# Four PSUM banks for the scores and one for the row maxima, formed in nine pieces, in a one-core attention and FFN kernel

## What is computed

```python
xn = _layernorm(x, axis=-1)
...
attn = jnp.einsum('bhqd,bhkd->bhqk', q, k) * scale
causal = jnp.triu(jnp.ones((Tx, Tx), dtype=bool), k=1)
attn = jnp.where(causal[None, None], -jnp.inf, attn)
attn = jax.nn.softmax(attn, axis=-1)
out = jnp.einsum('bhqk,bhkd->bhqd', attn, vh)
...
x = x + _L0_attn_ref(xn, ...) + _L0_ffn_ref(xn, ...)   # the FFN is quantised to 8 bits, with a gelu
```

## Time and profile before

| | us |
|---|---|
| median of 3 runs | 847.81 |
| lowest and highest | 843.24 and 855.21 |
| the profiled execution's own time | 854.1 |
| span of its trace | 852.3 |
| TensorE busy in the span | 768.1 (90%) |
| VectorE, ScalarE, GpSimd busy | 593.3, 494.2, 421.4 |

### The profile page before, as it was taken

The page is one execution under the profiler, slowest core; times in us unless marked ns, Lnnn a source line. Parts: engine busy times, 40 slices in busy tenths (PEclk is TensorE's granted clock), DMA queues, the critical chain, the costliest instruction groups (busy, mean ns, idle before and its releaser), DMA issues.

```text
span 852.3 us, 18026 instructions
## 1 busy us (share of the span) xinstructions
PE 768.1 (90%) x7038; PEld 580.5 (68%) x7038; DVE 593.3 (70%) x1534; ACT 494.2 (58%) x1005; POOL 421.4 (49%) x210
## 2 busy tenths in 40 slices
PE   4994776999999999999999999999999999999866
PEld 3672454667787778777877787778767876777635
DVE  7545985667676777667676767676766776776796
ACT  2541653666656665666466656565666566656753
POOL 3112661366654655555555555555566466640208
PEclk9766575999999999999999999999999999999978
DMA  9535134000100010001000100010000000000002
GB/s 279 169 123 197 50 123 149 2 14 14 39 14 2 2 26 3 14 13 39 14 1 2 28 1 14 15 41 12 1 5 24 1 3 2 1 2 2 13 1 99
DMA packets 20516, 33.07 MB, mean 39 GB/s; under 512 B 2704, under 2 KB 11472, under 8 KB 20304
## 3 DMA queue, kind: packets, MB, share of 16 engines
q1 hardware_dynamic: 19648, 31.34, 11.8%
q10 hardware_dynamic: 784, 0.59, 0.3%
HBM read 21.30 MB, written 10.49 MB: 37 GB/s over the span
## 4 chain that ended last, share of the span: by engine, by line
PE 45%; issue 25%; DVE 22%; ACT 6%; POOL 1%; DMA 1%; SPq 0%; POOLq 0%; DVEq 0%; ACTq 0%
PE psum L1045 40%; DVE p_lo L976 9%; ACT psum L670 3%; PE psum L1217 2%; DVE o_norm L877 2%; ACT p_hi L669 1%; POOL res L508 1%; DVE hid L1025 1%; DVE small L848 1%; DVE junk L848 1%; PE psum L1069 1%; ACT q_hi L594 1%; DVE small L996 1%; DMA acc<-in_L_attn_x 1%; DVE kt_a L941 1%
## 5 line engine op out<-in xcount | busy, mean ns | idle before, releaser
L669 ACT ACTIVATE p_hi<-psum 128x512 f16<-128x512 f32 (+3 forms) x384 | 187.5, 488 | 177.0 <-PE psum L1045 176.5
L848 DVE CUSTOM_DVE_ANT_0 junk<-psum,cmask 128x1024 bf16<-128x1024 f32 (+7 forms) x256 | 188.0, 753 | 129.8 <-issue 129.7
L976 DVE TENSOR_TENSOR p_lo<-psum,p_hi 128x512 f16<-128x512 f32 (+3 forms) x384 | 204.1, 552 | 57.8 <-ACT psum L670 57.5
L451 POOL TENSOR_TENSOR q_swap<-q_raw,sin_sb 32x1024 f32<-32x1024 f32 x31 | 73.3, 2365 | 267.0 <-ACT q_raw L590 266.9
L670 ACT ACTIVATE psum<-psum 128x512 f32<-128x512 f32 (+3 forms) x384 | 187.4, 488 | 0.0
L1045 PE MATMUL psum<-q_hi,k_hi 128*128 128x512 f32 (+2 forms) x384 | 164.3, 428 | 23.3 <-DVE p_lo L976 21.3
L1045 PEld LDWEIGHTS psum<-kv_tok,p_hi 128*128 128x128 f16 x2304 | 117.4, 96 | 37.6 <-issue 20.7
L1045 PE MATMUL psum<-kv_tok,p_hi 128*128 128x65 f16 (+1 forms) x2304 | 141.9, 195 | 0.4 <-DVE p_lo L976 0.4
L1045 PE MATMUL psum<-k_hi,q_hi 128*128 128x512 f32 (+3 forms) x384 | 123.8, 404 | 9.1 <-DVE small L848 9.1
L1045 PE MATMUL psum<-q_lo,k_hi 128*128 128x512 f32 (+2 forms) x384 | 132.0, 344 | 0.0
L1045 PE MATMUL psum<-q_hi,k_lo 128*128 128x512 f32 (+2 forms) x384 | 131.9, 343 | 0.0
(11 more groups left out here) (172 smaller groups left out, 1272.9 us busy)
## 6 DMA issues: line engine op xcount, KB each, us to landing
wq_split<-w_split SPq DMA_DIRECT2D x4, 1024.0 KB, 5.0
wq<-wq_split SPq DMA_DIRECT2D x16, 256.0 KB, 2.7
k_rotated<-k_split SPq DMA_DIRECT2D x8, 512.0 KB, 3.1
acc<-in_L_attn_x SPq DMA_DIRECT2D x4, 512.0 KB, 7.7
ffn_t<-in_L_attn_W_o SPq DMA_DIRECT2D x1, 2048.0 KB, 19.7
w_split<-in_L_ffn_w SPq DMA_DIRECT2D x2, 1024.0 KB, 6.0
k_hi<-k_rotated SPq DMA_DIRECT2D x8, 256.0 KB, 3.7
k_lo<-k_rotated SPq DMA_DIRECT2D x8, 256.0 KB, 4.3
```

What stands on the lines that cost most here:

```text
L451: pool.tensor_tensor(q_swap[0:HR, :], raw[HR:ROPE, :], sin_sb[HR:ROPE, :], ALU.mult)\
L669: act.activation(p_hi[j % PRING][:, o:o + used], src, ACT.Exp, scale=SCALE)
L848: ins = dve.tensor_tensor_reduce(junk[:, o:o + w], pmax[:, o:o + w], cmask[:, T - w:T], 1.0, LOWEST, ALU.add, ALU.max, mcol[:, s % 2, i:i ...
L976: dve.tensor_tensor(p_lo[j % PRING][:, o:o + used], score[c % SBANKS][:, w - used:w], p_hi[j % PRING][:, o:o + used], ALU.subtract).then_i ...
```

## The change

The scores get four banks, so chunk c uses bank c mod 4 and waits for the `p_lo` of chunk c-4. `pmax` shrinks to one bank. The units of maxima become nine pieces of at most 512 columns; a query tile of more than 512 columns is reduced in two pieces, the first of which leaves its result in the new tile `mpart`, from which the second goes on. `MAX_CHUNK` spreads the ten uses over the chunks of a step: after c0, c2, c3, c4, c5 and c6 the pieces u3 to u8 of step n+1, after c8 the transposition (u9), and after c9, c10 and c11 the pieces u0 to u2 of step n+2. In the preparation the ten uses stand in the seven passes as `FIRST_USES` says, two in the passes n = 2, 4 and 6, and three pieces of step 1 follow instead of two units.

```diff
-SBANKS, PRING = 3, 4
+SBANKS, PRING = 4, 4
...
-MAX_UNITS = [[(7, 0)], [(6, 0)], [(5, 0)], [(4, 0)], [(3, 0), (2, CH)], [(1, 0), (0, CH)]]
+MAX_UNITS = [[(7, 0, 0, CH)], [(7, CH, 0, CH)], [(6, 0, 0, CH)], [(6, CH, 0, 3 * P), (0, 0, 3 * P, P)],
+             [(5, 0, 0, CH)], [(5, CH, 0, 2 * P), (1, 0, 2 * P, 2 * P)], [(4, 0, 0, CH)],
+             [(4, CH, 0, P), (2, 0, P, 3 * P)], [(3, 0, 0, CH)]]
...
-MAX_SLOT = {0: (1, 2), 1: (1, 3), 2: (1, 4), 3: (1, 5), 5: (1, 6), 6: (2, 0), 7: (2, 1)}
...
+MAX_CHUNK = {9: (2, 0), 10: (2, 1), 11: (2, 2), 0: (1, 3), 2: (1, 4), 3: (1, 5), 4: (1, 6), 5: (1, 7), 6: (1, 8), 8: (1, 9)}
...
+FIRST_USES = ((0, 1), (2,), (3, 4), (5,), (6, 7), (8,), (9,))
...
-        score, pmax, head, misc = bank[0:3], psum[:, 3 * CH:5 * CH], bank[5:7], bank[7]
+        score, pmax, head, misc = bank[0:4], bank[4], bank[5:7], bank[7]
...
-                for i, o in MAX_UNITS[u]:
-                    w = (i + 1) * P
-                    ins = dve.tensor_tensor_reduce(junk[:, o:o + w], pmax[:, o:o + w], cmask[:, T - w:T], 1.0, LOWEST,
-                                                   ALU.add, ALU.max, mcol[:, s % 2, i:i + 1])
+                for i, k0, o, w in MAX_UNITS[u]:
+                    last = k0 + w == (i + 1) * P
+                    at = T - (i + 1) * P + k0
+                    if last and k0:
+                        dve.wait_ge(S["max_read"], USES * n + u)
+                    ins = dve.tensor_tensor_reduce(junk[:, o:o + w], pmax[:, o:o + w], cmask[:, at:at + w], 1.0,
+                                                   sm["mpart"][:, i:i + 1] if k0 else LOWEST, ALU.add, ALU.max,
+                                                   mcol[:, s % 2, i:i + 1] if last else sm["mpart"][:, i:i + 1])
...
-                pmax_use(0, 0, n - 2)
+                for u in FIRST_USES[n - 2]:
+                    pmax_use(0, 0, u)
...
-            for k in range(2):
+            for k in range(3):
                 pmax_use(1, 1, k)
...
-                            if c == (ENDS[j - 1] if j else 0) and j in MAX_SLOT:
-                                m, u = MAX_SLOT[j]
+                            if c in MAX_CHUNK:
+                                m, u = MAX_CHUNK[c]
...
-                        scores(n, s, j)
-                        if j in MAX_SLOT:
-                            m, u = MAX_SLOT[j]
-                            if n + m < LAST:
-                                if u == 0:
-                                    pe.wait_ge(S["qhi_done"], n + m + 1)
...
-                                pmax_use(n + m, s + m, u)
+                        for c in range(ENDS[j - 1] if j else 0, ENDS[j]):
+                            scores(n, s, c)
+                            if c in MAX_CHUNK:
+                                m, u = MAX_CHUNK[c]
+                                if n + m < LAST:
+                                    if u == 0:
+                                        pe.wait_ge(S["qhi_done"], n + m + 1)
...
+                                    pmax_use(n + m, s + m, u)
```

More of the change, by code:

```diff
@@ L74 @@
 ENDS = [max(c for c, x in enumerate(CHUNKS) if x[0] == j) + 1 for j in range(NT)]
[L75 removed]
+SBANKS, PRING = 4, 4
 LO_BASE = SBANKS
 assert NC % SBANKS == 0 and NT % PRING == 0
[L80 removed]
+MAX_UNITS = [[(7, 0, 0, CH)], [(7, CH, 0, CH)], [(6, 0, 0, CH)], [(6, CH, 0, 3 * P), (0, 0, 3 * P, P)],
+             [(5, 0, 0, CH)], [(5, CH, 0, 2 * P), (1, 0, 2 * P, 2 * P)], [(4, 0, 0, CH)],
+             [(4, CH, 0, P), (2, 0, P, 3 * P)], [(3, 0, 0, CH)]]
 NU = len(MAX_UNITS)
 USES = NU + 1
[L85 to L86 removed]
+MAX_CHUNK = {9: (2, 0), 10: (2, 1), 11: (2, 2), 0: (1, 3), 2: (1, 4), 3: (1, 5), 4: (1, 6), 5: (1, 7), 6: (1, 8), 8: (1, 9)}
+assert [u for _, u in sorted((m * -NC + c, u) for c, (m, u) in MAX_CHUNK.items())] == list(range(USES))
+FIRST_USES = ((0, 1), (2,), (3, 4), (5,), (6, 7), (8,), (9,))
 QHI_SLOT = 4
@@ L1161, in max_unit @@
                 pe.wait_ge(S["max_read"], USES * n + u)
[L1162 to L1169, removed]
+                for i, k0, o, w in MAX_UNITS[u]:
+                    ins = mm(pmax[:, o:o + w], q_hi[s % 4][:, i * P:(i + 1) * P], k_hi[b][:, k0:k0 + w], True, True)
                 ins.then_inc(S["max_done"], 1)
@@ L1178, in pmax_use, with scores @@
                       .then_inc(S["max_done"], 1)
-            def scores(n, s, j):
+            def scores(n, s, c):
                 b = s // REP
+                j, q0, w, used = CHUNKS[c]
                 ks = slice(j * P, (j + 1) * P)
-                for c in range(ENDS[j - 1] if j else 0, ENDS[j]):
-                    _, q0, w, used = CHUNKS[c]
-                    qs = slice(q0, q0 + w)
-                    o = score[c % SBANKS][:, 0:w]
-                    pe.wait_ge(S["lo_done"], NC * n + (c + 1))
-                    qh, ql = q_hi[s % 4], q_lo[s % 2]
-                    mm(o, k_hi[b][:, ks], qh[:, qs], True, False)
-                    mm(o, k_lo[b][:, ks], qh[:, qs], False, False)
-                    mm(o, k_hi[b][:, ks], ql[:, qs], False, False)
-                    if q0 + w - used == j * P:
-                        mm(o[:, w - used:w - used + P], cmask[:, T - P:T], ident[:, :], False, False)
-                    mm(o, ones_b[:, 0:P], m_row[s % 2][:, qs], False, True, S["score_done"])
+                qs = slice(q0, q0 + w)
+                o = score[c % SBANKS][:, 0:w]
+                pe.wait_ge(S["lo_done"], NC * n + (c + 1))
+                qh, ql = q_hi[s % 4], q_lo[s % 2]
+                mm(o, k_hi[b][:, ks], qh[:, qs], True, False)
+                mm(o, k_lo[b][:, ks], qh[:, qs], False, False)
+                mm(o, k_hi[b][:, ks], ql[:, qs], False, False)
+                if q0 + w - used == j * P:
+                    mm(o[:, w - used:w - used + P], cmask[:, T - P:T], ident[:, :], False, False)
+                mm(o, ones_b[:, 0:P], m_row[s % 2][:, qs], False, True, S["score_done"])
             def values(s, j, lo, read=None):
@@ L1295, in _ @@
             pe.wait_ge(S["qhi_done"], 2)
-            for u in range(2):
+            for u in range(3):
                 pmax_use(1, 1, u)
```

8 lines of the change are left out of this document (4 added, 4 removed).

## The result

The changed kernel takes 888.09 us (median of 4 runs, 881.09 to 892.80), beside 848.85 us for the kernel before on the same chip (843.24 to 855.21): a ratio of 1.045, 95% interval 1.035 to 1.056. It is slower by some 39 us. The profiled execution has a span of 879.3 us.

What follows compares the result with a forecast made beforehand. TensorE's list plus its waits bounds a step; the preparation is a chain through TensorE and VectorE. Attention +30 and preparation +6.5 give +36.5 us on the median 847.8, so 884 us; range 876 to 901, chance 0.62.

Steps and rivals of the forecast that it cites:

- What bounds the kernel: Attention: a step costs TensorE's list plus its waits, with 38.1 us of waits for `p_lo` before the scores.
- Part 1: Attention: with four score banks the bank waits before c3, c5 and c7 all go, -1.2 us a step, -38 us.
- Part 2: Attention: with one `pmax` bank u5 and u7 wait for VectorE, 1.48 us in plain and turn steps, 0.94 in out steps.
- Part 3: Attention: u0 after c9 waits 0.9 us for ScalarE's `q_hi`, paid in 30 steps.
- Part 4: Attention: VectorE's extra 0.8 us a step is free save within the handover; TensorE's fewer columns give -0.06 us a step.
- Sum of the attention: Attention: new waits against bank waits gone give +1.0 us a step, +30 us over the 30 full steps.
- Part 5: Preparation: second `pmax` uses hold up the keys products in passes 2, 4 and 6, +6.5 us, between 3 and 11.
- (a): Attention: VectorE is never behind, so only the least waits, 0.91 + 0.90 us a step, remain; 871 us, chance 0.20.
- (b): Attention: bank waits go and new waits are covered; 808 us in full (chance 0.05), 853 in mild form (chance 0.10).
- (c): Attention: TensorE's pauses make its clock fall, the sum is +58, 942 us; chance 0.03.

Runs made afterwards that it cites:

- three banks: The changed kernel with three score banks instead of four and still one bank for the maxima: 891.35 us, 1.050 of before.
- the pieces back in their slots: The kernel with two maxima buffers and three score banks, its nine pieces returned to the places of the kernel before: 865.99 us, 1.020 of before.
- the two-buffer kernel: The changed kernel with two banks for the maxima, used in turn, and three for the scores: 839.36 us, 0.988 of before.
- the split at the old places: The kernel before with only VectorE's reductions of more than 512 columns split in two: 860.31 us, 1.013 of before.
- the pair with three banks: The changed kernel with three score banks, with one maxima bank against two: 891.35 and 839.36 us.
- the first of the best kernels: The changed kernel with two maxima buffers, three score banks, `q_hi` in slot 3 and the reordered preparation: 813.48 us, 0.958 of before.
- the second: The changed kernel with two maxima buffers, three score banks, uses placed apart and the reordered preparation: 813.11 us, 0.956 of before.

## Why the prediction was right, step by step

The forecast was 884 us, the result is 888.09, within the range. Since the kernel with two buffers and early `q_hi` has none of the waits in question, each term can be measured on its own.

**What bounds the kernel.** As read: TensorE's list and its waits. In 599 us without waits TensorE is busy for 597.3.

**Part 1, the bank waits go: right in size, but not through the fourth bank.** Forecast 38 us and 2 more for fewer columns; the attention falls by 36.9 us from the kernel before (636.0) to the one without these waits (599.1). By periods 1.92, 1.13 and 0.09 us go in plain, turn and out steps, 1.07 on average where I had 1.2. The 0.66 us read as lost before c3 was low: from the recorded starts in the earlier trace rows it is 456.62 - 455.83 less the 0.03 of an unhindered start, 0.76. But I put the gain down to the fourth bank ("c3, c5 and c7 then need c(-1), c1 and c3"). With three banks they go too (three banks: 891.35 us, 3.2 us of idle time), and with the pieces back in their slots they are there with 53.1 us. It is the spreading of the reductions over the chunks that pays, and the bank taken from the maxima for the scores was spent for nothing. That the 38 us came out right is luck: the forecast counted the spreading only as a cost. Whether a fourth bank alone would have taken the waits away stays open. With the old two-bank units it needs a ninth bank; the nine pieces at the old places with four score banks and one `pmax` would have fitted, and were not run.

**Part 2, the handover: right.** Played through 1.48 us in plain and turn steps, 0.94 in out steps. The periods with one buffer and with two differ by 20.12 - 18.58 = 1.54, 21.17 - 19.77 = 1.40 and 25.17 - 24.24 = 0.93 (the two-buffer kernel has three score banks instead of four, which by the run with three banks changes no period by more than 0.02). The single waits fit too: 0.58 and 0.90 forecast in plain and turn steps and 0.63 and 0.90 found, 0.35 and 0.59 in out steps and 0.39 and 0.56 found. The Trainium skill (Perfetto Trace Analysis, Matmuls) says that independent matmul groups should rotate through different PSUM banks; for the maxima the runs agree, with 52.0 us for the second buffer. The scores rotate already, and a fourth bank in their turn changed nothing, with 891.35 us for three beside 888.09 for four.

**Part 3, u0 waits for q_hi: right.** 0.90 forecast, 0.90 to 0.92 measured by making `q_hi` earlier.

**Part 4, small terms: right where nothing waits for them.** 463.94 us of VectorE's work in 656 are no bound. But the split at the old places shows that the price is not nothing where a `p_lo` is waited for: 10.9 us.

**Sum of the attention.** +30 forecast, +30.9 measured: 36.9 go, 26.2 come back through `q_hi` and the rest of 67.8, 41.6, through the handover (41.9 by the pair with three banks).

**Part 5, the preparation: the mechanism right, the term too small.** 6.5 us forecast, 9.2 in the trace and 8.0 to 8.9 when the order is mended. Passes 2, 4 and 6 grow by 4.2, 4.2 and 4.4 us, where I had 3, 2 and 1.7; 2.9 are won back after pass 7, which nothing in the forecast foresaw. With the sums of VectorE as fast in both kernels (0.84 off pass 2, 2.15 back in pass 7), my estimate is 3.3 us in pass 2, close to the 3, and about 10.5 in all: the total is no further off because of a difference that the forecast did not have. The first step began at 137.09 and not near 149: I added the delay to the earlier trace rows as if all before it took the same time in every execution.

**The rivals.** (a), the floor alone: VectorE is behind: 0.86 us lie between the start of u4 and that of its reduction, where the floor has 0.42. (b), the freed banks win: the mechanism is real but needs a second buffer or other places for the uses; in the changed kernel the new waits are 2.2 us a step on average and not below 1.2. With two buffers, early `q_hi` and the reordered preparation the time is 813 us, near the 808 given for it. (c), the clock: it was granted at 1.00 in the steps, with three pauses of 0.6 to 0.9 us in each plain and turn step. The Trainium skill (TensorE: Matmul & The Clock Gate, "A second HAM failure mode: psum-queue depth-cycling") tells of a kernel in which short pauses between groups of matmuls made it fall. It gives no length for them; pauses as long as these did not do it here.

## What to carry to other kernels

Before a buffer is taken from one ring for another, find out what makes the ring that waits run late: here it was the order of VectorE's work, and a depth of three was enough once that was spread. With a buffer used in strict turns by two engines, each use waits for whatever the loop from start to start (here 1.6 us) exceeds the other work between two uses. Two buffers take that away, and so, for the most part, do other places for the uses (waits of 7.1 us are left of 34.5). A piece moved forward in one engine's list may overtake the engine that makes its input (`q_hi`): ask of each moved item who makes what it reads, and when.

## What the runs showed that I had not expected

**The start varies by 14 us between profiles.** Pass 2 on VectorE began between 89.8 and 104.2 us in the twelve profiles, although no instruction ahead of it was changed. Each kernel has one profile, so how much one kernel's own executions differ there is not shown. The granted clock differs too: from 20 to 85 us it is 0.68 in the kernel before and 0.76 in the changed one.

```profile
20.00:85.00 65.00, 50.53 (x193) 37.32 (x192) 34.45 (x58) 24.33 (x51) 11.66 (x13) 0.68 0.49 167
```
```profile
20.00:85.00 65.00, 46.57 (x218) 33.22 (x218) 45.77 (x70) 29.53 (x60) 20.17 (x17) 0.76 0.56 188
```

In the two-buffer kernel with the old slots it is 0.76 with pass 2 at 94.0, in the first of the best kernels 0.71 with 102.8, in the second 0.70 with 98.7, so the two go together only roughly. Whether the clock makes the start late or follows from it was not tested. A change in the preparation is to be read from one event to another, never from the two spans.

**A gap that is a missing record.** In the changed kernel's trace TensorE seems to pause 0.22 us before the transposition u9 in each step, which looks like one more wait. The page has 6964 matmuls and 7038 weight loads: 74 matmul records are missing, 71 of them of `psum<-m_row,ones_b`. With only the preparation reordered all 7038 are there, the gap is gone and the periods are the same to 0.05 us.
